# A two-layer network with a chunked scan: operands moved by 64 bytes, the step-size weights loaded a layer earlier, and a unit's four scans in one run

## What is computed

```python
x = layernorm(x + attention(x))            # layer 0
x = layernorm(x + sparse_ffn(x))           # layer 0
x = layernorm(x + ssm(x))                  # layer 1: most of the time
x = layernorm(x + ternary_ffn(x))          # layer 1

def ssm(h):
    gate, xBC, dt = split(h @ in_proj_w.T)           # 8192, 8192 + 2048, 128
    xBC = silu(depthwise_conv4(xBC) + conv_b)        # 4 taps along the tokens
    xs, B, C = split(xBC)                            # 128 heads of 64; 8 groups of 128 states
    dt = clip(softplus(dt + dt_bias))
    for each chunk of 128 tokens, head n, group g:
        y = (C B^T * exp(segment sums of dt * A)) @ (xs * dt) + carried state + D * xs
    yg = y * silu(gate)
    return (yg * rstd(per group) * norm_w) @ out_proj_w.T
```

## Time and profile before

| what | value |
|---|---|
| median of 3 runs | 2281.34 us |
| the profiled execution's own time | 2277.34 us |
| its span in the profile | 2275.5 us |
| TensorE busy | 2151.0 us (95%) |
| VectorE busy | 1584.5 us (70%) |
| ScalarE busy | 1191.1 us (52%) |
| GpSimd busy | 829.1 us (36%) |

### The profile page before, as it was taken

How to read it: one execution, slowest core, us unless ns; L and a number is a source line. 1 busy time by engine, 2 the same in 40 slices (tenths; PEclk the granted TensorE clock), 3 DMA queues, 4 the chain that set the end, 5 groups by cost and what they waited for, 6 DMA issues and landing times. The chain is left out here.

```text
span 2275.5 us, 38312 instructions
## 1 busy us (share of the span) xinstructions
PE 2151.0 (95%) x11176; PEld 1590.0 (70%) x11176; DVE 1584.5 (70%) x3186; ACT 1191.1 (52%) x2846; POOL 829.1 (36%) x680
## 2 busy tenths in 40 slices
PE   6899999997899999999999999999999999987998
PEld 4555555445677877877877777787787787766876
DVE  3666666645678599589589779858958958845345
ACT  4554545303566477377467557647737746642330
POOL 4352524211245245245335425514514533431230
PEclk9799999998999999999999999999999999998999
DMA  6000000003999487787777958868769777602100
GB/s 246 11 1 10 1 1 1 1 0 84 229 235 221 93 234 181 118 224 192 140 185 192 172 153 198 175 111 235 180 111 229 186 139 186 158 15 102 46 10 37
DMA packets 242996, 286.96 MB, mean 126 GB/s; under 512 B 9440, under 2 KB 211424, under 8 KB 242144
## 3 DMA queue, kind: packets, MB, share of 16 engines
q1 hardware_dynamic: 242784, 284.43, 52.6%
HBM read 281.78 MB, written 104.60 MB: 170 GB/s over the span
## 5 line engine op out<-in xcount | busy, mean ns | idle before, releaser
L1719 PE MATMUL b_ps<-xh_keep,wh 128*128 128x512 f32 x1152 | 473.9, 411 | 14.0 <-DVE xdt L1519 12.2
L1720 PE MATMUL b_ps<-xl_keep,wh 128*128 128x512 f32 x1152 | 457.1, 397 | 0.0
L1721 PE MATMUL b_ps<-xh_keep,wl 128*128 128x512 f32 x1152 | 457.1, 397 | 0.0
L1482 DVE SCALAR_TENSOR_TENSOR xs<-b_ps,par,xs 128x510 f32<-128x510 f32 (+2 forms) x384 | 285.0, 742 | 71.9 <-ACT xs L1205 54.1
L1393 POOL TENSOR_TENSOR wl<-wraw,wh 128x512 fp32r<-128x512 f32 x144 | 209.0, 1451 | 314.6 <-ACT wh L1184 314.6
L1510 DVE TENSOR_TENSOR decayed<-b_ps,b_scores 128x384 f32<-128x384 f32 x512 | 278.4, 549 | 49.1 <-ACT b_ps L1234 48.1
L1233 ACT ACTIVATE b_ps<-rows,ncs 128x256 f32<-128x256 f32 x512 | 238.1, 465 | 103.0 <-DMA rows<-skewed_rows 82.5
L1719 PEld LDWEIGHTS b_ps<-xh_keep,wh 128*128 128x128 f32 x1152 | 217.7, 189 | 86.2 <-issue 38.5
L1721 PEld LDWEIGHTS b_ps<-xh_keep,wl 128*128 128x128 f32 x1152 | 217.7, 189 | 52.3
L1405 POOL TENSOR_TENSOR yg<-yt,yg 128x512 f32<-128x512 f32 x112 | 147.1, 1313 | 292.8 <-DVE yt L1529 292.6
L1720 PEld LDWEIGHTS b_ps<-xl_keep,wh 128*128 128x128 f32 x1152 | 218.2, 189 | 45.0
(11 more groups left out here) (228 smaller groups left out, 3989.4 us busy)
## 6 DMA issues: line engine op xcount, KB each, us to landing
rows<-skewed_rows SPq DMA_DIRECT2D x256, 384.0 KB, 5.2
skewed_rows<-sum_rows SPq DMA_DIRECT2D x63, 1024.0 KB, 11.8
wraw<-win_dram SPq DMA_DIRECT2D x144, 256.0 KB, 6.0
skewed_rows<-sum_rows SPq DMA_DIRECT2D x63, 512.0 KB, 14.0
oraw<-wout_dram SPq DMA_DIRECT2D x8, 2048.0 KB, 15.5
w<-w_dram SPq DMA_DIRECT2D x2, 3584.0 KB, 23.2
fraw<-wgu_dram SPq DMA_DIRECT2D x11, 512.0 KB, 3.4
draw<-wd_dram SPq DMA_DIRECT2D x1, 2816.0 KB, 11.7
```

What stands on the lines that cost most here:

```text
L1482: ins = nc.vector.scalar_tensor_tensor(y[:, :, back:], z[:, :, 0:SEQ - back], param(g, sub, TAPS - 1 - back), y[:, :, back:], ALU.mult, AL ...
L1719: nc.tensor.matmul(out, w_h, x_h, start=(k == 0), stop=False)
L1720: nc.tensor.matmul(out, w_h, x_l, start=False, stop=False)
L1721: last = nc.tensor.matmul(out, w_l, x_h, start=False, stop=(k == KT - 1))
```

## The change

1. **Alignment.** The kept tensors are allocated in another order (the 64 bytes of `credit` ahead of x), so that `xh_keep` starts at byte 20608 and `xl_keep` at 36992, both multiples of 128. In `layer0` four small tensors (`st`, `bm`, `su`, `mn`) move to the end of the list.
2. **Step-size weights.** `wdt` and `dt_bias` are loaded by SyncE during layer 0 and split there (ScalarE `wdh` in the last stage, VectorE `wdl` behind it), into space that both layers share. The transposes of the last sequence's first tile (`back(3, 0)`) move into the last stage, into bank "v", and the two splits that follow them move ahead with them.
3. **Scans in one run.** TensorE's order in unit j becomes: X and G halves of unit j+1, scans 0 to 3 of unit j, turn(j+1). Y{j}_0 and Y{j}_1 are written to banks 0 and 1, the banks of the X halves; the two halves of a turn take banks 6 and 7. VectorE, ScalarE and SyncE follow in their orders: `skip` of half 1 stands at the head of the next unit, the fourth `decays` and `exps` move into their own unit, `load_rows` of the fourth sequence is issued one unit ahead like the other three, and in unit 7 the taps of C0 stand ahead of `skip(7, 0)`.

The core of the diff (the bank marks and SyncE's and most of ScalarE's order are left out; in this order the hunks are of the allocation, `mid_jobs`, layer 0's TensorE, SyncE, ScalarE and VectorE, then `ssm_layer`'s TensorE `steps`, VectorE `steps` and `crossing`, and the end of ScalarE's `steps`):

```diff
-        keep = {"x": sb("x_keep", [P, NT, HID]), "xh": sb("xh_keep", [P, KT, TOK], F32R),
-                "xl": sb("xl_keep", [P, KT, TOK], F32R), "consts": consts, "credit": sb("credit", [P, 16])}
+        keep = {"consts": consts, "credit": sb("credit", [P, 16]), "x": sb("x_keep", [P, NT, HID]),
+                "xh": sb("xh_keep", [P, KT, TOK], F32R), "xl": sb("xl_keep", [P, KT, TOK], F32R)}
...
             def mid_jobs(last):
             for j in range(UNITS):
-                out += [(f"T{j}_0", 6), (f"T{j}_1", 3), (f"Y{j}_0", 7), (f"Y{j}_1", 7)]
+                out += in_jobs(j + 1) if j < LAST else ([] if last else in_jobs(-1))
+                turned = [0] * (j == 0) + [j + 1] * (j < LAST)
+                out += [(f"T{n}_{h}", 6 + h) for n in turned for h in range(2)] + [(f"Y{j}_{h}", h) for h in range(2)]
...
                         outer(b, 3, (range(0, 4), range(4, FT0))[i])
+                        if b == BATCH - 1 and i == 0:
+                            back(b, 0)
...
+            sp.wait_ge(*bk.filled((BATCH - 1, "q", 1)))
+            sp.dma_start(wdt, io["wdt"]).then_inc(loaded["dt"], 16)
+            sp.dma_start(dt_bias, io["dt_bias"]).then_inc(loaded["dt"], 16)
...
+                    if b == BATCH - 1 and d == 1:
+                        act.wait_ge(loaded["dt"], 32)
+                        nc.scalar.activation(wdh, wdt, ACT.Copy).then_inc(dt_high, 1)
+                    if b == BATCH - 1 and d == 16:
+                        keep_high(b, 0)
...
+                if ffn is not None and b == BATCH - 1:
+                    dve.wait_ge(dt_high, 1)
+                    nc.vector.tensor_tensor(wdl, wdt, wdh.bitcast(F32), ALU.subtract)
+                    keep_low(b, 0)
...
             def steps(ph, g, last):
-                    turn(ph, j)
-                    if j:
-                        scan(ph, j - 1, 2)
-                        scan(ph, j - 1, 3)
+                    if not j:
+                        turn(ph, 0)
                     for name in names[2:4]:
                         in_half(ph, g, 5 + 2 * j, name)
-                    scan(ph, j, 0)
-                    scan(ph, j, 1)
+                    for b in range(BATCH):
+                        scan(ph, j, b)
+                    if not final:
+                        turn(ph, j + 1)
...
             def steps(ph, g, last):
...
-                    before, now = decays(ph, j - 1, 3), [decays(ph, j, b) for b in range(3)]
+                    d = [decays(ph, j, b) for b in range(BATCH)]
+
+                    def both(b):
+                        next(d[b])
+                        next(d[b])
+
                     if j:
-                        next(before)
-                        skip(ph, g, j - 1, 0)
+                        skip(ph, g, j - 1, 1)
+                        times_dt(ph, g, j, 0)
+                        times_dt(ph, g, j, 1)
+                        silu(ph, conv_halves(j)[2])
                         silu(ph, conv_halves(j)[3])
-                        next(before)
+                        both(0)
                         if h:
                             taps(ph, gn, h[0], (1, 2))
-                        next(now[0])
+                        both(1)
                         if h:
                             taps(ph, gn, h[0], (3,))
-                        next(now[0])
-                        times_dt(ph, g, j, 0)
-                        if h:
-                            silu(ph, h[0])
-                        next(now[1])
-                        times_dt(ph, g, j, 1)
-                        if h:
-                            taps(ph, gn, h[1], (1, 2))
-                        next(now[1])
-                        if h:
-                            taps(ph, gn, h[1], (3,))
-                        skip(ph, g, j - 1, 1)
+                        both(2)
                     else:
-                        taps(ph, gn, h[0], (1, 2))
                         scores(ph, 2)
                         scores(ph, 3)
+                        taps(ph, gn, h[0], (1, 2))
+                        both(0)
                         taps(ph, gn, h[0], (3,))
+                        both(1)
                         times_dt(ph, g, j, 0)
                         times_dt(ph, g, j, 1)
+                        both(2)
+                    if h:
+                        taps(ph, gn, h[1], (1, 2))
                         silu(ph, h[0])
-                        for b in (0, 0, 1):
-                            next(now[b])
-                        taps(ph, gn, h[1], (1, 2))
-                        next(now[1])
                         taps(ph, gn, h[1], (3,))
-                    next(now[2])
+                    both(3)
+                    if h and final:
+                        taps(ph, gn, h[2])
+                    skip(ph, g, j, 0)
                     if h:
                         silu(ph, h[1])
-                    if h and not final:
+                    if h and final:
+                        taps(ph, gn, h[3])
                         silu(ph, h[2])
-                    next(now[2])
-                    if h and final:
-                        taps(ph, gn, h[2])
                     if LAST - 2 <= j < LAST:
                         out_lo(ph, g, 0, LAST - 1 - j)
...
             def crossing(ph, g):
...
-                last_rows = decays(ph, LAST, 3)
-                next(last_rows)
-                skip(ph, g, LAST, 0)
-                next(last_rows)
-                silu(ph, bc_[2])
-                taps(ph, g + 1, bc_[3])
-                taps(ph, g + 1, h[0])
                 skip(ph, g, LAST, 1)
                 silu(ph, bc_[3])
+                taps(ph, g + 1, h[0])
                 taps(ph, g + 1, h[1])
                 silu(ph, h[0])
                 silu(ph, h[1])
...
                     if h and final:
+                        tap(ph, gn, h[2])
                         tanh(ph, h[1])
-                        tap(ph, gn, h[2])
+                        tap(ph, gn, h[3])
+                        tanh(ph, h[2])
                     elif h:
                         tanh(ph, h[1])
                         tanh(ph, h[2])
-                    next(now[2])
-                    if j:
-                        square(ph, j - 1, 1)
+                        tanh(ph, h[3])
                     if j == LAST - 2:
                         out_weights_hi(ph, g, 0)
                         out_hi(ph, g, 0, 1)
```

More of the change, by code:

```diff
@@ L219, in made, with dt_weights, layer0 @@
         return self.sem, self.at[name]
-def layer0(nc, sem, io, keep, cst):
+def dt_weights(shared, rounded):
+    wdt, wdh, wdl = (a[:, n * HID:(n + 1) * HID].rearrange("p (k h) -> p k h", h=P)
+                     for a, n in ((shared, 0), (rounded, 0), (rounded, 2)))
+    return wdt, shared[:, HID:HID + P], wdh, wdl
+def layer0(nc, sem, io, keep, shared, rounded, cst):
     with ExitStack() as ctx:
@@ L449, in back @@
                 pe.wait_ge(*x2_ready.made((b, t)))
-                transposes((b, "x2T", t), "y", [keep["x"][:, b * TPB + t, k * P:(k + 1) * P] for k in range(KT)])
+                transposes((b, "x2T", t), "v" if (b, t) == (BATCH - 1, 0) else "y", [keep["x"][:, b * TPB + t, k * P:(k + 1) * P] for k in range(KT)])
             pe.wait_ge(loaded["consts"], 16)
@@ L498, in _ @@
                         product((att, "wo", t), f"h{t}", HID, [(av[:, k, t * P:(t + 1) * P], wo[:, k, :]) for k in range(KT)])
-                if ffn is not None:
+                if ffn is not None and b < BATCH - 1:
                     back(b, 0)
@@ L664, in _ @@
                         act.wait_ge(*bk.filled((att, "av", u)))
-                        nc.scalar.activation(av[:, u, :], bk.out((att, "av", u)), ACT.Copy).then_inc(*bk.free((att, "av", u)))
-                if ffn is not None:
+                        nc.scalar.activation(av[:, u, :], bk.out((att, "av", u))[:, 0:SEQ], ACT.Copy).then_inc(*bk.free((att, "av", u)))
+                    if b == BATCH - 1 and d == 1:
[3 more added lines that the diff above has]
+                        keep_high(b, 0)
+                if ffn is not None and b < BATCH - 1:
                     keep_high(b, 0)
@@ L971, in ssm_layer @@
         wl = sb("wl", [P, RING, KT * P], F32R)
-        oraw = sb("oraw", [P, UNITS, HID])
-        oh = sb("oh", [P, 2, HID], F32R)
-        ol = sb("ol", [P, 2, HID], F32R)
+        oraw = shared[:].rearrange("p (n c) -> p n c", c=HID)
+        oh, ol = (rounded[:, n * 2 * HID:(n + 1) * 2 * HID].rearrange("p (n c) -> p n c", c=HID) for n in range(2))
         xs = sb("xs", [P, XSS, TOK])
@@ L996, in ssm_layer @@
         csT = yg[:, 5, :]
-        wdt = oraw[:, 0, :].rearrange("p (k h) -> p k h", h=NH)
-        wdh, wdl = (o[:, 0, :].rearrange("p (k h) -> p k h", h=NH) for o in (oh, ol))
-        dt_bias = oraw[:, 1, 0:NH]
+        _, dt_bias, wdh, wdl = dt_weights(shared, rounded)
         LAST = UNITS - 1
@@ L1012, in mid_jobs @@
             for j in range(UNITS):
```

(35 more changed lines are left out.)

70 lines of the change are left out of this document (31 added, 39 removed).

## The result

The changed kernel takes 2285.2 us (median of 20 runs) where the kernel before takes 2280.72 us (median of 20 runs): ratio 1.002, 95% interval 1.0012 to 1.0028. It is slower by 4.5 us, at the very edge of 0.2% but with the whole interval above no change, inside the stated range and on the side that was forecast, but by half of the 9 us forecast. One of the 20 runs of before took 6841 us; the other 19 lie between 2276 and 2287.

What follows compares the result with a forecast made beforehand. TensorE, busy 95% of the span, was taken as the bound, with VectorE next. Scans +19.6, early matmuls -0.65, step-size weights -4.8 and FFN alignment -4.9 gave +9.2, so 2290.5, rounded to 2290 us; range 2256 to 2316.

Steps and rivals of the forecast that it cites:

- the four new waits: TensorE waits per group at the turns (1.8 us), unit 7's turn (1.6), next X0 (2.3) and X1 (1.2): 6.9 together.
- I take the full difference: Alignment: every projection matmul goes from 0.2332 to 0.2264 us, 0.0068 less; 2.9 us a group, 4.9 in the FFN.
- 0.15 us a unit, 1.2 a group: Gain from one return from scans to projections per unit instead of two.
- scans, +42: Net price of the scans in one run by the prediction's terms: 51.7 us of waits less 9.6 gained.
- I cost both at nothing: Moved `load_rows` and the weights issued behind it on SyncE's queue cost no time, the cover being 15 us.
- the wait at X1: At the crossing, the next group's X1 waits for bank 1, that is for `skip(7, 1)`: 1.2 us.
- 4.8 was forecast: Step-size weights: 4.1 us from the new layer's earlier first matmul plus 0.7 from bank "v".
- The 0.7 of bank "v": Transposes at 520.67 no longer wait for the split that frees bank "y": 0.69 us less.
- VectorE did not keep ahead: Rival: VectorE keeps ahead and TensorE alone sets the time; 2239, or 2265 with half the waits; chance 0.29.
- `silu` of X1 was not held up by GpSimd: Rival: GpSimd holds up this `silu` in middle units, 0.85 us a turn; 2331, or 2304 in a third; chance 0.13.
- X0's 2.3 us: Next group's X0 waits for bank 0 because VectorE's unit 7 takes 17.1 us against TensorE's 14.9.
- 1.8 against 1.95 for the turns: Six turns a group each wait 0.3 us for `silu` of X1, behind `skip(j, 0)`: 1.8 us forecast.

Runs made afterwards that it cites:

- e1: The alignment alone (only the allocation order of the kept tensors) put into the kernel before: 2265.5 us, ratio 0.9938.
- e3: The changed kernel without the alignment (kept tensors in the old order): 2299.44 us, ratio 1.0084 to the kernel before.
- e14: The kernel before with only the 2 MB load of output weights moved from unit 1 to unit 3: 2269.63 us, ratio 0.9949.
- e10: Alignment and step-size weights in the old order of scans, output weights loaded in unit 3 instead of 1: 2249.54 us, ratio 0.9861 to the kernel before.
- e2: The kernel before with alignment and step-size weights, scans in the old order: 2259.78 us, ratio 0.9917.
- e5: The changed kernel with `silu` of X1 ahead of `skip(j, 0)` on VectorE in units 0 to 6: 2271.82 us, ratio 0.9964 to the kernel before.
- e13: The changed kernel with the fourth sequence's rows loaded as before, at the head of their own unit: 2287.78 us, ratio 1.0024 to the kernel before.
- e6: The changed kernel with `out_lo` of units 5 and 6 moved behind the next unit's first decays: 2272.17 us, ratio 0.9965 to the kernel before.
- e7: The changed kernel with the taps of C0 and C1 behind both skips of unit 7: 2281.11 us, ratio 1.0018 to the kernel before.
- e8: The changed kernel with earlier `silu` of X1, later `out_lo` and later taps of C together: 2254.57 us, ratio 0.9892 to the kernel before.
- e11: The changed kernel with those three VectorE edits and sums of squares three tiles later in the output projection: 2248.55 us, ratio 0.9854 to the kernel before.

## Why the prediction was right or wrong

The direction and the four new waits with their places were right, and so was the size of the waits as idle rows. The size of the total failed in two terms: the gain of the alignment was put some 13 us too high, and the price of the scans in one run some 18 us too high. The two errors nearly cancel, so it is luck that the total came within 5 us.

- **"I take the full difference" (alignment, -28.2).** The runs give -14 to -16: e1 against before, after against e3. In quiet groups without the wait for rows it is 182.75 (e14) - 180.8 (e10) = 1.95 instead of 2.9 us a group, since behind most switches from scans or transposes 5 to 11 matmuls keep the old distance. The 22 steps of the earlier trace rows came out of a uniform stream, and the earlier trace rows stands deep in one: neither shows what a switch does. In group 0 the gain was nothing (205.2 against 205.1). In the FFN the traces show 3 to 5 us, near the 4.9.
- **"0.15 us a unit, 1.2 a group", and what stands beside it (scans, +42).** The runs give +23 to +25 (after against e2). The gain was mis-sized: from e10's group, where no rows are waited for, 180.8 + 6.94 of waits + 0.37 (a tile of the output projection waits 0.72 instead of 0.35) would be 188.1, and after's quiet groups take 186.1, so 2.0 a group is left for the single run of scans and not 1.2. That is a net figure, since a wait costs more than its idle row (15.01 - 14.70 = 0.31 us for the 0.26 of a turn); where no turn waits, a middle unit gains 0.44 (e5). And 1.7 us a group (e14) of waits for rows went with the old order. The prediction says of the moved `load_rows` "I cost both at nothing"; e13 bears that out for the load itself, but the waits for rows that the old order had stand in no term. My first view was the stretch of one middle unit, and I took it for every unit of a group that took longer. The list of ScalarE's waits would have shown it. Group 0 went the other way, 3.5 to 5.3 us longer than in e2. The granted clock fell in three of after's groups 1 to 6, behind the wait at X0; that took up the wait at X1, and these groups lost only some 0.2 us by it.

**Step-size weights.** 4.8 was forecast, and e1 and e2 differ by 5.7, with intervals that overlap. The first matmul of the new layer starts at 524.66 in after (forecast 523.65, before 527.77), 1.3 behind the last split of x. The 0.7 of bank "v" did not show: the last transposes start at 520.78 instead of 520.67, since they now wait for `x_keep` itself.

```profile
520.78 1.12 PE L345 MATMUL a_ps<-consts,x_keep 128*128 128x128 f32 x4 [4.54 <-DVE x_keep L812]
```

e1 moves the operands by 64 bytes, and the settled distance falls from 0.233 to 0.2265. The rule of the Trainium skill, TensorE: Matmul & The Clock Gate, "Wait — 56ns, not 53.3ns?", by which the distance goes by columns and clock alone, does not hold here. Its figure of 215.7 ns was reached in no stream here.

**The rivals.** VectorE did not keep ahead. `silu` of X1 was not held up by GpSimd: over all X halves, first and second, the mean of `silu` fell from 1108 ns to 898, by the two groups of before and of after,

```profile
L1492 DVE SCALAR_TENSOR_TENSOR xs<-tx,xs 128x512 f32<-128x512 f32 x128 | 141.3, 1108 | 9.2 <-ACT tx L1221 9.2
```

```profile
L1504 DVE SCALAR_TENSOR_TENSOR xs<-tx,xs 128x512 f32<-128x512 f32 x128 | 115.0, 898 | 4.5 <-ACT tx L1240 4.5
```

and of the 64 second halves of after, on which the turns wait, 49 take 0.7 us; in 47 of these GpSimd starts its operation only while the `silu` runs.

**Right by a wrong step.** The prediction builds X0's 2.3 us from 2.0 for `out_lo` in unit 7, 2.2 for the taps of C0, and -0.7 and 0.5 that no row is given for. Without that `out_lo` the wait falls only from 2.4 to 1.9 (e6), and with the taps of C0 and C1 behind the skips it is gone (e7). So that one figure came out right by terms that were wrong.

## What to carry to other kernels

Count a loop's gain from the whole loop, not from its quietest turn: list every engine's waits over the full period first, since a change can take away a wait that is not its subject, or be paid back by one. A gain per instruction that was read deep in a uniform stream holds, in these traces, only some instructions behind most switches. Where a chain of handovers is laid out row by row, its waits can be forecast closely (1.8 against 1.95 for the turns), but a figure that comes out right does not prove its terms: take each away in a run. And each wait taken away can show the next one (e7, e8, e11).

## What was not expected of the hardware

- Behind most switches from scans or transposes the aligned matmuls run 0.224 to 0.240 apart (about 0.232 in the mean) for 5 to 11 steps, then 0.2265; unaligned ones alternate between 0.231 and 0.236 throughout. What sets the length was not tried.
- An idle time of 1.35 us (e7) was followed by matmuls at half the clock, though TensorE was busy again in between. This happened in four of groups 1 to 6 and not in the other two, which had the same wait.
- One 2 MB load issued two units earlier on the same queue cost 11.9 us of 2281 (e14). In e2, which has the same early load, the rows of the decays came 1.85 and 2.58 us after ScalarE was free for them.
